# First products of two rotated projections put into the attention in front, and a turned item copied last on ScalarE

## The reference, cut to what matters

```python
# L0_ffn: rms(x) @ wq -> 32 heads of 64, @ wk, @ wv -> 8 heads; queries and keys rotated
q, k = q * cos + rot(q) * sin, k * cos + rot(k) * sin
# L1_xattn: 16 query heads and 4 key heads of 128
q = _rms_norm((draft_hidden @ Wq.T).reshape(bsz, draft_len, H, HD), q_norm_w)   # mean square over each head
k = _rms_norm((kv_in @ Wk.T).reshape(bsz, total_len, KVH, HD), k_norm_w)
v = (kv_in @ Wv.T).reshape(bsz, total_len, KVH, HD)
q, k = _rope(q, draft_position_ids), _rope(k, full_position_ids)
```

## Time and profile before

| | us |
|---|---|
| median of 3 runs | 2730.29 (2729.73 to 2731.96) |
| profiled execution | 2728.3 |
| its span | 2726.6 |
| TensorE busy | 2479.4 (91% of the span) |
| VectorE busy | 1704.5 (63%) |
| ScalarE busy | 1154.6 (42%) |
| GpSimd busy | 934.5 (34%) |

### The profile page before, as it was taken

One profiled execution on the slowest core, in us unless ns is written; L12 is line 12 of the kernel. 1 busy time (PEld: TensorE's weight loads), 2 busy tenths in 40 slices (PEclk: granted clock), 3 DMA queues, 4 the chain that ended last, 5 costly groups with the idle time before them and its releaser, 6 DMA issues. The chain is left out here.

```text
span 2726.6 us, 48715 instructions
## 1 busy us (share of the span) xinstructions
PE 2479.4 (91%) x14967; PEld 2033.7 (75%) x14968; DVE 1704.5 (63%) x3211; ACT 1154.6 (42%) x2389; POOL 934.5 (34%) x943
## 2 busy tenths in 40 slices
PE   7999788879899999799997998997999998999998
PEld 7888666658688887588875886665777787888887
DVE  4536847769777666676675566866555535666564
ACT  2103256623343334455553233757655522444443
POOL 4203201134333234423333212753333312355554
PEclk9999989989899989899998988998999989999999
DMA  5544122125622055477774432444222131666664
GB/s 191 154 140 114 28 93 77 46 91 168 179 68 65 15 166 182 147 220 223 195 223 105 131 68 96 151 125 126 73 70 72 55 129 63 182 163 159 147 163 73
DMA packets 304547, 336.59 MB, mean 123 GB/s; under 512 B 149231, under 2 KB 220063, under 8 KB 302578
## 3 DMA queue, kind: packets, MB, share of 16 engines
q1 hardware_dynamic: 233170, 256.24, 30.1%
q0 software_dynamic: 20640, 51.74, 9.7%
q10 hardware_dynamic: 50560, 26.34, 3.3%
HBM read 235.70 MB, written 98.56 MB: 123 GB/s over the span
## 5 line engine op out<-in xcount | busy, mean ns | idle before, releaser
L898 PE MATMUL e_psum<-e_up_hi,hT_hi 128*128 x672 | 244.9, 365 | 14.5 <-DVE hT_lo L867 11.0
L900 PE MATMUL e_psum<-e_up_hi,hT_lo 128*128 x672 | 237.0, 353 | 0.0
L899 PE MATMUL e_psum<-e_up_lo,hT_hi 128*128 x672 | 236.4, 352 | 0.0
L1938 POOL TENSOR_TENSOR joint_a_p<-joint_a_p,joint_a_rinv 112x487 f32<-112x487 f32 x128 | 125.5, 1002 | 187.5 <-DVE joint_a_rinv L1992 187.1
L1569 POOL TENSOR_TENSOR self_a_p<-self_a_p,self_a_mx 112x448 f32<-112x448 f32 x96 | 96.1, 1002 | 205.8 <-DVE self_a_mx L1626 205.8
L898 PEld LDWEIGHTS e_psum<-e_up_hi,hT_hi 128*128 128x128 f32 x672 | 127.6, 190 | 34.7 <-issue 24.5
L794 ACT ACTIVATE e_gate<-e_psum 128x352 f32<-128x352 f32 (+1 forms) x86 | 44.5, 517 | 247.0 <-PE e_psum L900 246.6
L1997 DVE TENSOR_REDUCE joint_a_mx<-joint_psum 112x1 f32<-112x487 f32 x128 | 84.9, 663 | 101.4 <-PE joint_psum L1963 100.7
L873 DVE TENSOR_TENSOR hT_lo<-e_psum,hT_hi 128x256 fp32r<-128x256 f32 (+2 forms) x138 | 55.7, 435 | 144.8 <-ACT hT_hi L812 144.8
L1660 ACT ACTIVATE self_a_p<-self_a_p 112x448 f32<-112x448 f32 x128 | 71.6, 574 | 168.1 <-POOL self_a_p L1569 114.9
L1211 POOL TENSOR_TENSOR p_p_z<-p_p_straight,p_p_crossed 128x512 f32<-128x512 f32 x70 | 98.4, 1407 | 112.5 <-DVE p_p_crossed L1193 110.5
(11 more groups left out here) (574 smaller groups left out, 7483.0 us busy)
## 6 DMA issues: line engine op xcount, KB each, us to landing
e_up_raw<-in_L_ffn_w SPq DMA_DIRECT2D x64, 512.0 KB, 5.0
e_up_raw<-in_L_ffn_w SPq DMA_DIRECT2D x64, 352.0 KB, 4.1
e_dn_raw<-in_L_ffn_w SPq DMA_DIRECT2D x16, 1024.0 KB, 5.5
q_all<-p_p_t_stage ACTq DMA_DIRECT2D x56, 256.0 KB, 2.3
e_dn_raw<-in_L_ffn_w SPq DMA_DIRECT2D x16, 512.0 KB, 6.3
x_first<-q_all SPq DMA_DIRECT2D x32, 224.0 KB, 2.7
v_ctx<-front_c_v_stage SPq DMA_DIRECT2D x24, 250.0 KB
x_others<-k_ctx SPq DMA_DIRECT2D x8, 750.0 KB, 5.3
```

The lines of the kernel that those rows point to most:

```text
L898: pe.matmul(out, lhs[0], rhs[0], start=k == 0, stop=False)
L899: pe.matmul(out, lhs[0], rhs[1], start=False, stop=False)
L900: return pe.matmul(out, lhs[1], rhs[0], start=False, stop=k == n_k - 1)
L1938: pool.tensor_tensor(p[:, r, 0:S], p[:, r, 0:S], rinv[:, r:r + 1].to_broadcast([T, S]), ALU.mult).then_inc(p_ready, 1)
```

## The change

The eight PSUM banks are now held over two segments: one tensor for cross1 and p2, one for self3 and p4. A new part, `BegunProductsPart`, lives in the attention segments on TensorE alone: for one item it issues 11 of the 12 matmuls of the first weight block and leaves out the last, high by low of slice 3. `RopeQkvPart` issues only that last one for the first `begun` items. Five items are begun in cross1 (banks 0 to 3 and 6, so p2 works with five banks instead of four), three in self3 (of the banks 2, 3, 6, 7). Before the first begun item TensorE waits for all four slices of the split weights, for the attention to have left the banks, and for the tokens of enough batches.

In cross1's list the loads of `FirstWeightPart` now begin 12 entries in front of the attention's last one, and no longer near the list's end. And in `RopeQkvPart` ScalarE's copy of the turned item is moved behind the square and the scale. The part of the tensor generator and the moved lines:

```diff
-        R, LR, MM_BANKS, T_BANKS = 3, 3, (0, 1, 2, 3), (4, 5)
+        R, LR, MM_BANKS, T_BANKS = 3, 3, mm_banks, t_banks
@@ RopeQkvPart.tensor
-                    products(pe, ps[:, MM_BANKS[step % len(MM_BANKS)], :], lambda k: (core.hT_hi[:, k, tok], core.hT_lo[:, k, tok]),
-                             lambda k: weight(n, k), KC).then_inc(mm_done, 1)
+                    out = ps[:, MM_BANKS[step % len(MM_BANKS)], :]
+                    if step < begun:
+                        pe.matmul(out, core.hT_lo[:, KC - 1, tok], first[0][:, KC - 1, :], start=False, stop=True).then_inc(mm_done, 1)
+                    else:
+                        products(pe, out, lambda k: (core.hT_hi[:, k, tok], core.hT_lo[:, k, tok]), lambda k: weight(n, k), KC).then_inc(mm_done, 1)
@@ RopeQkvPart.scalar: this block moved from in front of the square to behind the scale
                 i = step - LR
                 if 0 <= i < n_rot:
                     n, t = i // TT, i % TT
                     act.wait_ge(z_used, i + 1)
                     reuse(act, t_stored[i % 3], 16 * (i // 3))
                     src = ps[:, T_BANKS[i % len(T_BANKS)], :].rearrange("p (c t) -> p c t", c=4)
                     act.activation(t_stage[:, i % 3, :, :], src, ACT.Copy).then_inc(t_ready, 1)
                     act.wait_ge(t_ready, i + 1)
...
+class BegunProductsPart:
...
+        def tensor(pe):
+            for t, bank in enumerate(banks):
+                tok, out = slice(t * 128, (t + 1) * 128), ps[:, bank, :]
+                may_begin(pe, t)
+                for k in range(KC):
+                    pe.matmul(out, core.hT_hi[:, k, tok], hi[:, k, :], start=(k == 0), stop=False)
+                    pe.matmul(out, core.hT_hi[:, k, tok], lo[:, k, :], start=False, stop=False)
+                    if k < KC - 1:
+                        pe.matmul(out, core.hT_lo[:, k, tok], hi[:, k, :], start=False, stop=False)
+                yield
@@ cross1
+                    def may_begin(pe, t):
+                        if t == 0:
+                            pe.wait_ge(f.ready, KC)
+                            pe.wait_ge(a.exp_done, B * 16)
+                            pe.wait_ge(o.ht_ready, B - 2)
+                        if rope_banks[t] == 6:
+                            pe.wait_ge(a.o_evac, B)
+                    last_a = len(order) - order[::-1].index("a")
+                    order[last_a:] = ["begun"] * 2 + order[last_a:last_a + 2] + ["begun"] + order[last_a + 2:last_a + 6] + ["begun"] * 2 + order[last_a + 6:]
+                    loads = last_a - 12
+                    g.run(["landed"] + order[:90] + ["f"] + order[90:loads] + [n for name in order[loads:last_a] for n in (name, "f")] + order[last_a:])
@@ self3
+                        if t == 0:
+                            pe.wait_ge(f.ready, KC)
+                            pe.wait_ge(a.o_evac, B * a.evacs_per_group)
+                            pe.wait_ge(o.ht_ready, 4)
+                order[-8:] = order[-8:] + ["begun"]
+                order[-5:-5] = ["begun"]
+                order[-10:-10] = ["begun"]
```

More of the change, by code:

```diff
@@ L1049, with __init__ @@
 class RopeQkvPart:
-    def __init__(self, g, name, half, eps, wq, wk, wv, q_to, k_to, v_to, q_tables, k_tables, tables_from, first, last_stores):
+    def __init__(self, g, name, half, eps, wq, wk, wv, q_to, k_to, v_to, q_tables, k_tables, tables_from, first, last_stores, mm_banks, t_banks, begun):
         core, ps = g.core, g.ps
@@ L1166, in scalar @@
                     last.then_inc(z_ready, 1)
+                i = step - LR
+                if 0 <= i < n_rot:
+                    n, t = i // TT, i % TT
+                    act.wait_ge(z_used, i + 1)
+                    reuse(act, t_stored[i % 3], 16 * (i // 3))
+                    src = ps[:, T_BANKS[i % len(T_BANKS)], :].rearrange("p (c t) -> p c t", c=4)
+                    act.activation(t_stage[:, i % 3, :, :], src, ACT.Copy).then_inc(t_ready, 1)
+                    act.wait_ge(t_ready, i + 1)
+                    to = q_to[n * D:(n + 1) * D] if n < 4 else k_to
+                    act.dma_start(to[:, t * 128:(t + 1) * 128].rearrange("(c p) t -> p c t", p=128),
+                                  t_stage[:, i % 3, :, :]).then_inc(t_stored[i % 3], 16)
                 yield
@@ L1221, in __init__ @@
         g.part(name, sync=sync, tensor=tensor, scalar=scalar, vector=vector, gpsimd=gpsimd)
+class BegunProductsPart:
+    def __init__(self, g, name, first, banks, may_begin):
+        core, ps = g.core, g.ps
+        hi, lo = first
+        def tensor(pe):
[8 more added lines that the diff above has]
+                yield
+        g.part(name, tensor=tensor)
 class QkvPart:
@@ L3525, in decoder @@
                     g.run(order[:keys_at] + ["x"] + order[keys_at:queries_at] + ["x"] + order[queries_at:])
-                with Segment(core, "cross1") as g:
+                hold_ps = ExitStack()
+                cross_ps = hold_ps.enter_context(nc.psum_tensor("cross_psum", [128, 8, 512], F32))
+                rope_banks = (0, 1, 2, 3, 6)
+                with Segment(core, "cross1", cross_ps) as g:
                     a = CrossAttentionPart(g, "a", lambda b: q1[b], lambda b: [(slice(0, C), k_ctx[b])],
@@ L3582, in decoder @@
             first = hold_first.enter_context(nc.sbuf_tensor("x4_first", [128, 2, KC, D], F32R))
-            with Segment(core, "self3") as g:
+            hold_ps = ExitStack()
+            self_ps = hold_ps.enter_context(nc.psum_tensor("self_psum", [128, 8, 512], F32))
+            rope_banks = (2, 3, 6, 7)
+            begun = 3
+            with Segment(core, "self3", self_ps) as g:
                 n = FirstNormPart(g, "n", (2, 3), rows=acc, late=1, holds=(lambda sp: sp.wait_ge(p.lora_lo_ready, 1), lambda sp: sp.wait_ge(p.lora_added, KC)))
@@ L3614, in decoder @@
                                 (tabs[0], tabs[1]), (tabs[2], tabs[3]), [(t, tok_tabs[k]) for k, t in enumerate(tabs)],
-                                (first[:, 0, :, :], first[:, 1, :, :]), last_values)
+                                (first[:, 0, :, :], first[:, 1, :, :]), last_values, rope_banks, (4, 5), begun)
                 f = FirstBatchPart(g, "f", p, [
```

34 lines of the change are left out of this document (16 added, 18 removed).

## The result

The changed kernel takes 2713.39 us (median of 5 runs, 2711.99 to 2716.03), the kernel before 2730.29 (five runs, 2727.25 to 2733.26). The ratio is 0.9939, with a 95% interval of 0.9924 to 0.9953. The profiled execution has a span of 2711.6 us, 15.0 less than before.

The account below looks back on a forecast made before the run. It took p4 as bound by a ring of turn, copy, square and scale, with no engine full. Cross1 +0.5, p2 -4.1, self3 +1.2, p4's head +0.6, steps -12.9: -14.7, 2713.6, plus 2.0 for the median: 2716 us (2708 to 2724).

Parts of the forecast that it names:

- p4's steps: Second rotated projection: copying last cuts a ring of engine waits, 29 steps from 3.65 to 3.19 us; net -12.9 us.
- p4's head: Start of p4: TensorE idles while the rotation tables come, so its next product runs cold; +0.6 us, bounds 0 and 2.4.
- self3's tail: End of self3: the last 11 begun matmuls stand behind the last turn, hidden by no wait; +1.2 us.
- p2's head: Start of p2: VectorE's waits of 1.04, 1.43, 0.30 and 1.32 us go; -4.1 us, bounds 0 and -5.3.
- Its 5.20 stays: Start of p2: VectorE still starts with the tables, so its 5.20 us wait for them remains.
- cross1, +0.5: End of cross1: late weight slices delay oT_hi 1.9 us, a warmer TensorE clock gives -2.0; together 0.5 us later.
- (a): Rival, cross1 and self3: tails cost nothing, weights land in time and the clock stays full; 2712 us, chance 0.17.
- (b): Rival, p4: the step falls only to 3.4 us because ScalarE has no room; 2722 us, chance 0.15.
- (c): Rival, p4: the ring isn't what holds 3.65 us, so the new order changes nothing; 2729 us, chance 0.05.
- (d): Rival, cross1, self3 and p4's head: begun products run at 1.2 GHz, making the kernel slower; 2736 us, chance 0.03.

Follow-up runs that it names:

- e1: Kernel before with one edit: ScalarE copies the turned item behind the squares and scale in both rotated projections; 2715.3 us, ratio 0.9955.
- e2: Changed kernel with the copy put back ahead of the squares and scale, both sets of begun products kept; 2725.9 us, ratio 0.9995.
- e3: Changed kernel without the three begun products in self3's tail; 2713.2 us, ratio 0.9940 to the kernel before.
- e12: Changed kernel with 36 unused matmuls on TensorE in p4 ahead of item 0's turn; 2712.4 us, ratio 0.9946 to the kernel before.
- e4: Changed kernel without cross1's five begun products, the first weights' loads and splits staying at its earlier place; 2721.8 us, ratio 0.9976.
- e5: Changed kernel with p2's first weight slices loaded and split up to twelve loop steps earlier and two steps apart; 2718.3 us, ratio 0.9961.
- e7: Changed kernel with one product begun in self3's tail, not three; 2711.8 us, ratio 0.9935 to the kernel before.
- e8: Changed kernel with p4's query tables loaded and waited for first, the keys' pair behind the weight blocks; 2711.1 us, ratio 0.9935.
- e10: Changed kernel with one product begun in self3 and p4's query tables first (e7 and e8 together); 2710.2 us, ratio 0.9931.
- e11: e10 without cross1's begun products and with the loads of p2's first weights at their old place; 2712.0 us, ratio 0.9938.

## Why the prediction was right

The forecast was 2716 (2708 to 2724), the measured median 2713.4. Of the 2.6 us between them 2.0 are the offset that was added for the median: the profiled execution's own sum was 2713.6, and its time (span and 1.8 us around it) is 2713.4. So close a hit is partly luck, as the steps show, though the mechanism is the one forecast:

- **p4's steps, forecast -12.9.** Right in cause (e1, e2); -13.8 in the trace, 33 steps by 0.42. I counted 29 steps from item 3 on, and held back 0.4 for ScalarE behind the weight halves. From 1711 to 1800 its square still waits 0.50 to 0.97 us for the product in 17 of its steps, and TensorE never for the scale, so that reserve wasn't needed. (ScalarE's 22.0 per seven steps is 22.1 when added again, which changes nothing.)
- **p4's head, +0.6.** Mis-sized: the first step alone is 1.9 us longer than before. I charged a part of the cold product; all 12 matmuls but the last few ran at half clock, near the upper bound (2.4). Tables and item 0's chain give 0.7 back, so the head is +1.2. Against e1, where TensorE doesn't wait for item 0, the changed kernel's p4 part is 3.5 us worse, and against e3 3.1. Of those 3.1, 1.3 are self3's tail and 2.3 the first step, and the earlier tables give 0.6 back. The begun products buy nothing there while the tables come last, as the prediction said, but they also take away the work that kept the clock up.
- **self3's tail, +1.2.** Measured 1.3, in six traces with three begun products alike: 2.3 us from VectorE's last step to the tables' issue, against 1.0.
- **p2's head, -4.1.** The sum fits (-4.1 here, -3.5 to -5.2 in seven traces), its parts don't. "Its 5.20 stays" was wrong: it is 3.42 now, since the second table itself lands sooner. Its issue, size and median time to landing, before and after:

```profile
f_sin<-in_rope_sin SPq DMA_DIRECT2D x1, 224.0 KB, 4.4
```

```profile
f_sin<-in_rope_sin SPq DMA_DIRECT2D x1, 224.0 KB, 2.7
```

In the nine traces with begun products in cross1 it takes 2.7 or 2.8 us, 3.5 in e12; in the four without them 3.8 to 4.7. The four also show an instruction fetch of 16 KB among the transfers of these microseconds, and the nine don't; whether it holds up the table isn't shown. Item 0's own product was close behind as a candidate: before, its last matmul starts at 581.94 and is printed to end at 582.33, 0.4 ahead of the table, and in e4 it comes last (5.03), 0.5 behind the table. So both had to come sooner for the 1.8 us. What I missed on the other side is the second weight block: its landing is the new wait, 2.06.
- **cross1, +0.5.** The slices were late as forecast (waits of 1.34 and 1.09, oT_hi 2.0 late; 1.9 forecast), and alone cost 3.1 (e4; the bounds were 0 and 3.5). The row from which the fetch was taken held: these slices landed in 3.0 us at the least. By an estimate from the fixed cost alone, near 2 us, which the Trainium skill states in "DMA: Bandwidth & Descriptors" where it tells where the 2 us go, oT_hi would have been 1 us less late than it was; the traces don't bear that out. What the begun products give back differs from execution to execution, and with it the granted clock. Seven traces have this code. In four p2 starts at -0.2 to +0.2 against cross1's loop, in three at +1.4 to +2.4. But the four gained 0.6 to 0.7 near 521, ahead of the loads and in code that the change leaves alone; against the loop behind that place they stand at +0.6 to +0.9, the changed kernel at +0.8, and the three at +1.3 to +2.4. So the forecast +0.5 is met within 0.3 either way, and not closer than the place from which one counts. The last 18 to 20 us before p2, TensorE's clock in the last column but two, of the changed kernel:

```profile
core 0: us, PE busy (x) PEld busy (x) DVE busy (x) ACT busy (x) POOL busy (x), PEclk, DMA share, GB/s
559.00:577.30 18.30, 12.39 (x59) 9.07 (x57) 10.01 (x20) 1.63 (x3) 4.54 (x5) 1.00 0.00 1
```

and of e3:

```profile
core 0: us, PE busy (x) PEld busy (x) DVE busy (x) ACT busy (x) POOL busy (x), PEclk, DMA share, GB/s
560.60:580.84 20.24, 14.40 (x58) 10.43 (x56) 10.36 (x20) 1.63 (x3) 4.89 (x5) 0.85 0.00 1
```

The four have 1.00, the three 0.85 to 0.87. Why one execution keeps the clock and another doesn't stays open.

Of the rivals, (a) was nearer in number (2712) for the wrong reasons: neither tail was free. (b) and (c) fell with the steps of 3.21. (d) was partly there, in p4's first whole product, but in none of the changed kernel's begun matmuls; in e3, e5, e7 and e8 one to four of cross1's start 0.40 to 0.43 us apart. My trust in the sum was too good: its errors in p4's steps (0.9) and head (0.6) went opposite ways, and parts that the change doesn't touch scatter by 6.7 us between profiled executions (the last expert stage gives back between -0.8 and +5.9).

The lowest median is e10's, 2710.2 us; its interval overlaps the changed kernel's, so only the traces (5.1 us less in p4's part, 0.9 of them from the gap that its one begun product fills in self3) speak for it.

## What to carry to other kernels

In a step where one engine serves both ends of a ring, do first what needs only the product in front, and last what needs the partner's answer: that gained 14 us here with no instruction added. Work begun early pays only where it is what comes last, or where it fills a gap (0.9 us in e7, e10 and e11). Ask at the same time what it leaves the engine to do in the next wait: behind the 9.17 us that the changed kernel's TensorE stood idle, the next product started at half clock. Where the releaser that the trace names and another candidate end within a few tenths (0.4 us in p2's head), taking away one alone would gain only that. And before you price a part from one trace, look at which microseconds hold the gain: half of e7's 4.5 lay in front of the place that the edit was meant for.

## What the runs showed of the hardware

A wait printed as 0.20 us on TensorE made a step 0.42 us longer. The last matmul of a product in the kernel before, in front of the turning at 1742.33:

```profile
1741.74 0.39 PE L142 MATMUL p_psum<-p_p_w_hi,hT_lo 128*128 128x512 f32 x1
```

The two start 0.59 us apart; after the change 1726.34 and 1726.57, 0.23 apart. That is 0.36 of the 0.42, and the turning itself takes the rest (0.41 to the next matmul's start, then 0.35). The print counts from a modelled end, so compare starts.

The granted clock was at half behind an idle time of 2.54 us (e7) and still full behind those of 1.37 (e10) and 1.83 us (e12). It decides more than p4's head: output products of self3 start 0.43 us apart in e3 and 0.23 in e10, and the same code near 1662 took 1.5 us less in one of 13 executions.

Landings of one transfer scatter: p4's four tables were in 7.3 to 8.4 us behind their first issue in ten executions, and the two query tables alone in 4.7, 5.7 and 6.1 in three.
